# A list scheduler's table of phase lengths, DMA landings and priority offsets replaced by another, in a hybrid attention and expert kernel on one core

## What is computed

```python
def attention_a(x):      # local: 16 heads of 16, 44 offsets (0 to 40, 96, 128, 384)
    scores = einsum('bhtd,bhtjd->bhtj', q, k[t - offset] * (1 + scale_embed)) / 4 + pos_bias
    return (softmax(scores) @ v[t - offset]) * if_gain @ w_out
def attention_b(x):      # full causal attention, 16 heads of 16, with biases
    return softmax(causal(Q @ K.T / 4)) @ V @ Wo + bo
def experts(x):          # top 2 of 8 experts
    cont = sigmoid(x @ enc_W + enc_b) @ s2c_W + s2c_b
    gates = normalised top 2 of softmax(tanh(cont @ rW1 + rb1) @ rW2 + rb2)
    moe = sum_e gates[e] * (relu(cont @ We1[e] + be1[e]) @ We2[e] + be2[e])
    return layernorm(sigmoid(sigmoid(moe @ c2s_W + c2s_b) @ dec_W + dec_b)) * ln_g + ln_b
x = x + attention_a(layernorm(x));  x = x + experts(layernorm(x))
x = x + attention_b(layernorm(x));  x = x + experts(layernorm(x))
```

## Time and profile before

| | |
|---|---|
| three timed runs | 1747.72, 1752.73, 1756.09 us, median 1752.73 |
| the profiled execution's own time | 1755.84 us |
| its span, first to last instruction | 1753.8 us (2.0 us lie around it) |
| TensorE (PE) busy | 1584.8 us, 90% |
| VectorE (DVE) busy | 1278.3 us, 73% |
| ScalarE (ACT) busy | 791.3 us, 45% |
| GpSimd (POOL) busy | 133.0 us, 8% |
| mean granted TensorE clock | 0.972 of full speed |

### The profile page before, as it was taken

One profiled execution on the slowest core, in us unless ns is written; L12 is line 12 of the kernel. 1 busy time (PEld: TensorE's weight loads), 2 busy tenths in 40 slices (PEclk: granted clock), 3 DMA queues, 4 the chain that ended last, 5 costly groups with the idle time before them and its releaser, 6 DMA issues. The chain is left out here.

```text
span 1753.8 us, 28230 instructions
## 1 busy us (share of the span) xinstructions
PE 1584.8 (90%) x10544; PEld 884.8 (50%) x10560; DVE 1278.3 (73%) x3138; ACT 791.3 (45%) x1474; POOL 133.0 (8%) x155
## 2 busy tenths in 40 slices
PE   5689899998999989999899999999899998997976
PEld 2163564545655465554654556454655446554533
DVE  5968856896588956788568975789667986656723
ACT  1133445535364543644455353544435443553533
POOL 1020110001101020000200001000100001000000
PEclk8998999999999999999999999999999999998988
DMA  9040450014300152020700235001530206004000
GB/s 320 21 158 14 150 153 2 16 73 169 87 2 23 66 181 74 4 86 8 230 19 2 86 108 148 2 15 73 179 76 3 74 27 210 20 20 128 15 1 12
DMA packets 50261, 133.96 MB, mean 76 GB/s; under 512 B 6256, under 2 KB 22576, under 8 KB 45520
## 3 DMA queue, kind: packets, MB, share of 16 engines
q1 hardware_dynamic: 50128, 132.16, 23.2%
HBM read 80.99 MB, written 46.04 MB: 72 GB/s over the span
## 5 line engine op out<-in xcount | busy, mean ns | idle before, releaser
L1306 DVE TENSOR_TENSOR arena_AB<-qT,kT 128x2048 f32<-128x2048 f32 (+3 forms) x240 | 400.3, 1718 | 20.7 <-PE bank L1632 14.3
L1361 DVE CUSTOM_DVE_ANT_0 bank<-bank,causal_b 128x512 f32<-128x512 f32 (+3 forms) x512 | 233.6, 527 | 85.2 <-PE bank L1697 84.6
L1543 PE MATMUL bank<-arena_F,kept 128*128 128x512 f32 x512 | 238.8, 616 | 5.7 <-DVE arena_F L1451 2.9
L1625 PE MATMUL bank<-arena_AB,slot_w 128*32 128x512 f32 x1408 | 200.2, 617 | 42.2 <-DVE arena_AB L1306 40.7
L1135 ACT ACTIVATE arena_AB<-bank 128x512 f32<-128x512 f32 (+1 forms) x352 | 167.7, 596 | 65.8 <-PE bank L1713 65.7
L1168 ACT ACTIVATE arena_F<-bank,kept 128x512 f32<-128x512 f32 x256 | 157.5, 700 | 15.3 <-PE bank L1543 13.5
L1543 PEld LDWEIGHTS bank<-arena_F,kept 128*128 128x128 f32 x512 | 97.4, 197 | 119.5 <-issue 104.4
L1821 PE MATMUL bank<-kept,arena_F 128*128 128x256 f32 x512 | 117.0, 382 | 7.4 <-ACT arena_F L1185 5.5
L1806 PE MATMUL bank<-arena_F,kept 128*64 128x512 f32 x512 | 121.5, 602 | 1.2 <-ACT arena_AB L1135 0.3
L1543 PE MATMUL bank<-cont_hi,by_cont 128*128 128x512 f32 (+1 forms) x272 | 113.9, 419 | 9.4 <-DVE arena_AB L1361 7.2
L1543 PE MATMUL bank<-xnT,kept 128*128 128x512 f32 x256 | 116.4, 604 | 2.3 <-issue 0.9
(11 more groups left out here) (186 smaller groups left out, 2350.3 us busy)
## 6 DMA issues: line engine op xcount, KB each, us to landing
arena_AB<-band SPq DMA_DIRECT2D x32, 1344.0 KB, 7.1
...
```

Of the source, the lines that this page charges most:

```text
L1306: ins = nc.vector.tensor_tensor(prod[SET_AT[i]][:, col:col + c, :], qT[:, hf, :].unsqueeze(1).broadcast_to([P, c, T]), k, ALU.mult)
L1361: ins = nc.vector.tensor_tensor_reduce(out=s, in0=s, in1=causal[:, (TT - 1 - i) * P:T], scale=-1.0, scalar=BIG, op0=ALU.add, op1=ALU.min, ...
L1543: ins = nc.tensor.matmul(out(ps), w, x, start=n == 0, stop=n == len(pairs) - 1)
L1625: ins = nc.tensor.matmul(ps[HS * col:HS * (col + 1), :], slot_w[:, slot(n), :], prod[SET_AT[i]][:, col, :], start=r == 0, stop=False, skip ...
```

## The change

Only numbers are changed: lengths of blocks, the landings of DMAs, the earliest starts, `CLOCK` (a divisor of TensorE's lengths), `DEPTH`, and the offsets. No instruction is added or taken away, and each line keeps its own order. The greedy scheduler gives another interleaving on TensorE, VectorE and ScalarE; on SyncE's queue the order of the steps is the same, and on GpSimd one step moves (A2's `pow` ahead of A1's third far term). A few lines of each kind:

```diff
-    p.put("xn", ("DVE", 1.3, ("pow", "POOL")))
+    p.put("xn", ("DVE", 1.35, ("pow", "POOL")))
...
-            p.put(("write", i), ("SP", 0.4, ("p", i, "ACT")), ("DMA", 2.2))
+            p.put(("write", i), ("SP", 0.4, ("p", i, "ACT")), ("DMA", 2.6))
...
-                                        *([("pB", k - 2, 1, "PE")] if k >= 3 else [])), ("DMA", 6.3))
+                                        *([("pB", k - 2, 1, "PE")] if k >= 3 else [])), ("DMA", 7.0))
...
-            p.put(("oT", i), ("PE", 1.35 if i > 0 else 0.86, *needs), ("ACT", 0.48))
+            p.put(("oT", i), ("PE", 1.46 if i > 0 else 1.02, *needs), ("ACT", 0.6))
...
-        p.put(("tanh", n), ("ACT", 0.6, ("dec", n, "DVE")))
+        p.put(("tanh", n), ("ACT", 1.1, ("dec", n, "DVE")))
...
-        p.put("store", ("SP", 0.4, ("close", "DVE")), ("DMA", 4.0))
-        p.put("load", ("SP", 0.4, ("store", "DMA")), ("DMA", 4.0))
+        p.put("store", ("SP", 0.4, ("close", "DVE")), ("DMA", 7.0))
+        p.put("load", ("SP", 0.4, ("store", "DMA")), ("DMA", 5.0))
...
-LOAD, CLOCK = 0.1, 0.95
-TICK, DEPTH = 0.02, 1.61
+LOAD, CLOCK = 0.1, 1.0
+TICK, DEPTH = 0.02, 1.55
...
-    ("F", "PE"): {"turn": 190, "hid": 750, "eo": 1320, "dec": 5540},
+    ("F", "PE"): {"turn": -620, "hid": 316, "eo": 1710, "dec": 10230},
...
-    "A": [-4350, 0, 0, 0, 0, 0, 0, 170],
+    "A": [-7420, 0, 0, -510, -460, -300, -60, -157],
...
-RELEASE = {(ATTENTION[0], "stats"): 4.2, (ATTENTION[0], "xn"): 7.6, (SETUP, "slots"): 10.2, (SETUP, "small"): 60.0}
+RELEASE = {(ATTENTION[0], "stats"): 4.9, (ATTENTION[0], "xn"): 8.1, (ATTENTION[1], "stats"): 24.0,
+           (ATTENTION[3], "stats"): 30.0, (SETUP, "slots"): 11.5, (SETUP, "small"): 60.0}
```

More of the change, by code:

```diff
@@ L141, in output_phases @@
             on_needs[0].append(("oNT", i - 2, "PE"))
-        p.put(("on", i), ("PE", 0.44, *on_needs[0]), ("DVE", 1.3 if far else 0.63, *on_needs[1]))
+        p.put(("on", i), ("PE", 0.42, *on_needs[0]), ("DVE", 1.3 if far else 0.63, *on_needs[1]))
     elif kind == "oNT":
-        p.put(("oNT", i), ("PE", 0.22, ("on", i, "DVE"), *([("pr", i - 2, "PE")] if i >= 2 else [])), ("ACT", 0.26))
+        p.put(("oNT", i), ("PE", 0.25, ("on", i, "DVE"), *([("pr", i - 2, "PE")] if i >= 2 else [])), ("ACT", 0.26))
     else:
-        p.put(("pr", i), ("PE", 0.86, ("oNT", i, "ACT")), ("DVE", 0.34 if far else 0.8))
+        p.put(("pr", i), ("PE", 0.78, ("oNT", i, "ACT")), ("DVE", 0.36 if far else 0.9))
 def local_phases():
@@ L168, in local_phases @@
             needs.append(("prod", USED_BY[q], "PE"))
-        p.put(("prod", q), ("DVE", 0.067 * len(runs(q)) + 0.534 * len(of), *needs), ("PE", 0.86 if r < 3 else 1.12 if g == NG - 1 else 0.98))
+        p.put(("prod", q), ("DVE", 0.067 * len(runs(q)) + 0.534 * len(of), *needs), ("PE", 0.9 if r < 3 else 1.3 if g == NG - 1 else 1.1))
         if r == 3:
@@ L225, in raw @@
     def raw(h, n):
-        p.put(("S", h, n), ("PE", (0.22, 0.23, 0.12)[n], ("stack", h // 4, "DMA")), ("DVE", (0.62, 0.76, 0.37)[n]))
+        p.put(("S", h, n), ("PE", (0.2, 0.25, 0.1)[n], ("stack", h // 4, "DMA")), ("DVE", (0.64, 0.76, 0.38)[n]))
     def maxima(hf):
@@ L231, in turn_maxima @@
     def turn_maxima(hf):
-        p.put(("mT", hf), ("PE", 0.24, ("mx", hf, "DVE")), ("ACT", 0.46), ("SP", 0.4), ("DMA", 4.5))
+        p.put(("mT", hf), ("PE", 0.32, ("mx", hf, "DVE")), ("ACT", 0.6), ("SP", 0.4), ("DMA", 4.5))
     def turned_scores(n, m):
@@ L245, in weigh @@
         g, k = STEPS[n]
-        p.put(("PV", n), ("PE", (0.86, 0.64, 0.43, 0.23)[k], *[("ST", n, m, "ACT") for m in range(len(SHARE[k]))],
+        p.put(("PV", n), ("PE", (1.0, 0.78, 0.6, 0.37)[k], *[("ST", n, m, "ACT") for m in range(len(SHARE[k]))],
                           *([("v", m, "DVE") for m in range(2)] if n == 0 else [])))
@@ L281, in expert_phases @@
     p.put("rh", ("PE", 0.46, ("cont", "DVE")), ("ACT", 0.6))
-    p.put("lg", ("PE", 0.9, ("rh", "ACT")), ("DVE", 2.85))
+    p.put("lg", ("PE", 1.0, ("rh", "ACT")), ("DVE", 2.93))
     for kind, n in EXPERTS:
@@ L290, in expert_phases @@
             if n == 5:
-                p.put("ln_b", ("DVE", 1.14, ("xn", "DVE")))
+                p.put("ln_b", ("DVE", 1.25, ("xn", "DVE")))
         elif kind == "gT":
-            p.put(("gT", 0), ("PE", 0.24, ("gates", "DVE")), ("ACT", 0.46))
+            p.put(("gT", 0), ("PE", 0.32, ("gates", "DVE")), ("ACT", 0.7))
         elif kind == "gb":
@@ L298, in expert_phases @@
             needs = [("hid", 4 * n + k, "ACT") for k in range(4)]
-            p.put(("eo", n), ("PE", 1.72, *needs), ("DVE", 0.67 if n == 0 else 1.4, ("gb", n, "ACT")))
+            p.put(("eo", n), ("PE", 1.87, *needs), ("DVE", 0.67 if n == 0 else 1.52, ("gb", n, "ACT")))
     for m in range(KF):
@@ L303, in expert_phases @@
         p.put(("dec", n), ("PE", 3.43, *[("c2s", m, "ACT") for m in range(KF)]), ("DVE", 0.61))
[L304 to L305 removed]
+        p.put(("tanh", n), ("ACT", 1.1, ("dec", n, "DVE")))
+    p.put("stats_2", ("DVE", 2.1, ("tanh", 0, "ACT"), ("tanh", 1, "ACT")))
     p.put("pow_2", ("POOL", 1.0, ("stats_2", "DVE")))
[L307 removed]
+    p.put("close", ("DVE", 3.4, ("pow_2", "POOL"), ("ln_b", "DVE")))
     if layer == 1:
[L309 to L310 removed]
+        p.put("store", ("SP", 0.4, ("close", "DVE")), ("DMA", 7.0))
+        p.put("load", ("SP", 0.4, ("store", "DMA")), ("DMA", 5.0))
     return p.table
```

17 lines of the change are left out of this document (7 added, 10 removed), and 4 rows, old and new, of the table CALL_PULL.

## The result

| | before | changed |
|---|---|---|
| median of six executions each | 1752.90 us | 1737.05 us |
| lowest and highest | 1747.72 to 1756.09 | 1734.03 to 1739.92 |
| ratio, 95% interval | | 0.991, 0.9897 to 0.9923 |
| profiled execution, own time (span) | 1755.84 (1753.8) | 1734.03 (1731.9) |
| mean granted TensorE clock in it | 0.972 | 0.977 |

The change is worth 15.9 us, 0.9%. The spans of the two profiled executions differ by 21.9 us, 6 more than the medians, because the one of before is among its slowest and the changed one is its fastest. Term by term only these two can be compared, so what follows explains 21.9 us, and some 6 of them are the draw of the executions.

The account below looks back on a forecast made before the run. TensorE, busy 1584.8 of 1753.8 us, was taken as the bound, with its idle and half-clock time at stake. The terms summed to -4.1 us, taking the median from 1752.7 to 1748.6 us; range 1733 to 1765.

Parts of the forecast that it names:

- Start -5.0: A0: `slots` no longer waits for x_second, so the third product set starts earlier; 5.0 us saved (bounds -9.0 and 0).
- A1 +3.5: A1: `dec` 0 moves ahead of `tS`, so `pA` 0 waits some 6 us; 3.5 us lost (bounds 0 and +6).
- Ends, waits -20.7: Ends of A2 to A6: TensorE's waits before `oT` go, 27.7 us, less 7.0 of new ones; net 20.7 us saved.
- Seams, waits +21.5: Seams of A2 to A6: new TensorE waits around `oNT`, B's first `S` and `turn`, 4.3 us each; 21.5 us lost.
- The 2.6 before B's first `S`: Seams of A2 to A6: TensorE waits 2.6 us for the stack, held behind a load awaiting the store's landing.
- Clock -15.3 and +12.5: A2 to A6: half-clock stretches at the ends go, 15.3 us saved; new ones in the seams cost 12.5 us.
- Elsewhere -2: After the seams: VectorE does B's `S` maxima during projections, perhaps shortening later waits; 2 us saved (bounds -10 and +3).
- A7 -0.9: A7: `pr` 0 covers half of the 1.72 us wait; 0.9 us saved.
- B6 +2.3: B6: `lo` and `v` 1 ahead of `on` 0 delay `oNT` about 3 us, 0.7 regained; 2.3 us lost.
- The seams' cheap case: Seams of A2 to A6 cost 1.9 us each without half clock: 1724 us, or 1736 halfway; faster, chance 0.36.
- The load in front of the stacks: SyncE's queue, A2 to A6: the load before the stacks becomes the bound, 10.0 us a seam, 1769 us; chance 0.20.
- It does not do what it says: Something other than `stats` may hold the last `pB` copies: sum +7.6, 1760 us; within the 0.44 for no difference.

Follow-up runs that it names:

- e2: Kernel before, with the next A call's `stats` behind `on` 2 instead of ahead of tile 3's `pB` copies, in A2 to A6: 1756.31 us, ratio 1.0012.
- e3: Kernel before, with TensorE's second `dec` (`dec` 1) behind tile 0's `pA` products in A2 to A6: 1795.27 us, ratio 1.024.
- e4: Kernel before, with `close` behind `on` 0 instead of ahead of tile 1's `pB` copies in A2 to A6: 1753.35 us, ratio 1.0006.
- e9: Kernel before, with only the phases of the ends of A2 to A6 in the changed kernel's order: 1768.36 us, ratio 1.0093.
- e11: Changed kernel, with earlier `turn` and later `stats`, `xn` in A2 to A6's seams, A1's `dec` back before `pA`, last-seam steps moved: 1729.54 us, ratio 0.9871.
- e5: Changed kernel, with the next A call's `stats`, `xn`, `turn`, `qk` and `v` back ahead of B's first `S` in A2 to A6: 1790.85 us, ratio 1.0213.
- e10: Changed kernel, with the phases of the ends of A2 to A6 in the order of before: 1750.04 us, ratio 0.998.

## Why the prediction was right and wrong

The sum said -4.1 against the profiled execution; it was -21.9.

- **Start -5.0 and A1 +3.5.** Measured at the ends of `oT` 3: -6.8 in A0, of which A1 gives back 2.4 (240.6 to 236.2 in all). The third set starts at 25.55 (27 forecast), `oT` 0 stands at 96.86 (97), `pA` 0 waits 5.74 (6). The rows are right. The net, -4.4 against a forecast of -1.5, is in good part the draw of the two executions: in the other profiles A1 ends between 237.8 and 240.3 with the old start (e2, e3, e4, e9) and between 236.2 and 238.6 with the new one (the kernel before had 240.6): so the start is worth 1 to 2 us, net of what A1 gives back, as forecast.
- **Ends, waits -20.7.** Measured -23.0. Right as a sum, and the earlier trace rows was read rightly: e2 and e9 show `stats` holding the copies. Wrong was the reading that each wait goes by its own move and takes its time with it. e2, e3 and e4, one move each, brought nothing, a loss of 41 us, and nothing: in e2 and e4 the wait went and came back at the next step, in e3 it doubled.
- **Seams, waits +21.5.** Measured +14.4, 2.9 a seam instead of 4.3. The 2.6 before B's first `S` was the failed step: it took the 9.54 us of the earlier trace rows for the price of a landing and carried it over to a store that the change issues elsewhere. Issued 6 us behind the last band read, a store lands in 3.0 (after, e4), and the wait for the stack was 0.4 to 0.9. The trace of the kernel before had it already: F12's store of the earlier trace rows, to which the prediction compared this one, also stands 6 us behind the last band read, and its row (DMA issues, 1470 to 1476 us: KB, us to landing) is

```profile
out<-x_third SPq DMA_DIRECT2D x1, 512.0 KB, 3.1
```

  The rest of the seam was taken a little low: 0.77 around `oNT` for 0.9, but 0.31 and 1.33 for VectorE to empty banks around `turn` for 0.8.
- **Clock -15.3 and +12.5.** By the same measure -15.4 (12.1 in the ends and 3.3 behind them) and +6.8. Two mistakes are in it: the seams lost less, and the measure was priced one to one. Over the 14 profiles of this study, with the same instructions, TensorE's busy time runs from 1576.2 us at a clock measure of 33.6 (e11) to 1599.3 at 66.2 (e3; e5 has 1594.4 at 74.8), and a straight line through them rises by 0.52 us per us (correlation 0.94; 0.54 with the missing records added). By that fit the clock terms were worth half. Why is not shown; part of a half-clock window may be idle or not slowed.
- **Elsewhere -2.** Measured -2.9 (A1 to A2), +1.8 (`tS` to `oT` 0) and -5.5 (middles): -6.6, within its bounds and three times its value. In the middles the rows are L1625 waiting for VectorE's products, 11.5 to 8.3 us, and several small waits for VectorE that go (for B's maxima and for xn, 4.6 us together), against 2 us of new ones. Of the 9.3 us by which L1625's whole row falls (40.7 to 31.4), 5.5 lie in A0 and belong to the start. e10's middles hold 21.6, e9's, with B's old order, 33.4, so the gain comes from that half. That VectorE is ahead later because it does B's first maxima while TensorE projects fits these rows but was not tried by itself.
- **A7 -0.9 and B6 +2.3.** The wait before `oT` 2 of A7 fell from 1.72 to 0.84. B6's 3.01 is there, 1.3 of it regained at the next turn. The two rows are right; with smaller waits beside them the stretches gave -1.0 together (-1.7 and +0.7), not +1.4.
- **Rivals.** The seams' cheap case gave 1724 to 1736, and the time came out just above. "The load in front of the stacks" did not occur: the load left 5 us before the stack. A slow store issued as late as the change issues it was not tried. "It does not do what it says" is refuted by e2.

Of the 17.8 us between forecast and profile, 7.1 are the seams' waits, 4.6 the elsewhere, 2.3 the ends, 2.4 A7 and what follows it, 0.7 the start, and the rest the busy time. All err to the same side, and some 6 us are the draw of the executions. That the median still lies in the range is owed to the range's width, which held the half-cheap seams, and not to the seams' price, which was wrong.

The prediction cited "TensorE: Matmul & The Clock Gate", Part 1, of the Trainium skill, that the ramp penalty is under 1% of a span. Here the lost clock by my measure is 49.0 us, 2.8%, before and 38.9, 2.2%, after, so for this kernel the traces speak against it; with the factor of 0.52 its cost is 1.4% and 1.2%.
